# Macaron block on one core: the router with high and low weights side by side as one operand

## The chip, the cores and the metric
One core of one Trainium2 chip. The metric is the device time of one execution in microseconds. Before the change the median of 3 runs is 681.12 us (680.85 to 681.37).

## The reference, cut to what matters
The input x has 16 sequences of 256 tokens with 128 features. It passes through an FFN with a mixture of experts, a mixer (gated convolution and linear recurrence), and the same FFN again, each behind a layer norm and added to x. The part that the change touches is the router of the FFN:

```
logits = tokens @ router_weight.T          # [T, 128] x [128, 32]
scores = sigmoid(logits)
sfc    = scores + router_bias
# two best groups of 8 experts by the sum of their two best; 4 best experts in them
topk_w = scores of the 4, divided by their sum, times 2.5
```

All 32 experts (64 hidden units each) and a shared expert are computed for each token, and an expert's output is weighted by topk_w or by zero.

## The kernel before, in words
**Precision.** Every float32 operand of a large product is split into a high part in fp32r and a low part, the rest. A product is three passes: high with high, high with low, low with high. So it is for the router: for each of the four groups of 128 tokens in a block of 512 it issues three products (L1178 to L1180), with the tokens as the stationary operand and the router's weights, 32 columns, as the moving one; twelve in all, into the PSUM bank `side`.

**Units and slots.** A block is 512 tokens, 8 blocks in all. A unit is one FFN on one block, (1, b) for the first FFN and (4, b) for the second. `ORDER` lists the 16 units: (1,0) to (1,3), then (4,0), (1,4), (4,1), (1,5), (4,2), (1,6), (4,3), (1,7), (4,4) to (4,7). I number them 0 to 15 in that order. A unit has 17 tiles j = 0 to 16 (`NT`): the shared expert and 16 pairs of experts. For a tile TensorE makes a group of three products into `gate_ps` and one into `up_ps` (L1094 to L1096, two banks of each), ScalarE takes silu of gate_ps (L669), VectorE multiplies by the routing weights (`weighted`, L827) and by up_ps (`hid`, L840), ScalarE makes the high part of hid (L677), GpSimd the low part (L562), and TensorE makes three down products (L1152 to L1155), three tiles later. `up_tiles` waits for `hid_done` of tile n-2 before the up group of tile n, and for `weighted_done` of tile n-2 before its gate group.

**Side work.** All that is not a tile is work "beside" it: layer norms, transposes, the router, the routing steps, the mixer, output sums. Tables written by hand (`PREPARE`, `ROUTE4`, `BEGIN`, `END` and others, L315 to L409) give each step a slot: slot 5 on VectorE is between weighted and hid of tile 5, slot 5.5 behind hid of tile 5 (`beside`, L986). On TensorE slot 5 comes behind the tile's up and down products, on ScalarE behind silu of tile 5 and the high part of tile 4. Every engine executes its own list in order. Regular units are those that the tables `MIXER`, `ROUTE4`, `OUTPUT`, `NEXT` describe for (1, b), which route for the second FFN, and `NORM4`, `PROJECT`, `ADD`, `PREPARE` for (4, b), which route for the first FFN.

**The routing chain.** In slot 2 or 3 TensorE runs the router. VectorE then makes 26 small steps (`route_step`, L878), each waiting for the one before: a step away from zero for the logits, reciprocal, score (silu of the logits from ScalarE times the reciprocal), bias, best of groups, ranks, top 8, match_replace, and last `w_tok` (L953). `even(first, last)` spreads them over the half slots. TensorE transposes w_tok (`transpose_route`, L1185), ScalarE copies it (`wT_copy`, L704), and SyncE stores it and broadcasts it to all partitions for the next unit.

**One bank for all.** The PSUM bank `side` serves all side work of TensorE in turn; before a new use TensorE waits until the last one has been read (`side_read`). For the router that is step 2 of the routing chain (`LOGITS_READ`).

**Setup.** Before the units the weights are loaded, transposed and split, and block 0 is routed. The first routing steps lie on VectorE before the low part of batch 3.

Of the kernel before, what the change touches and what calls it, by code (L numbers as in the profile page):

```python
# [111 lines left out]
def macaron_kernel(nc, x, W_in, conv_w, conv_b, a_param, W_out, ln_w, ln_b, router_w, router_b,  # L112
# [4 lines left out]
    with ExitStack() as ctx:  # L117
# [17 lines left out]
        side_te = side_td[:, :, 0:E]  # L135

# [75 lines left out]

        tiny = sb("tiny", [P, TT, E])
# [3 lines left out]
        score = routed[:, 0:128].rearrange("p (t e) -> p t e", t=TT)  # L217
        biased = routed[:, 128:256].rearrange("p (t e) -> p t e", t=TT)
# [56 lines left out]
        logits_ready = {k: sem(f"logits_ready{k}") for k in (1, 4)}  # L275
        logit_silu_done = {k: sem(f"logit_silu_done{k}") for k in (1, 4)}
# [27 lines left out]
        ROUTE = 26  # L304
# [5 lines left out]
        def even(first, last, n=ROUTE):  # L310
# [10 lines left out]
        PREPARE = {"transpose 1": 0, "xT high 1": 1, "xT low 1": 1, "router 1": 2, "silu logits 1": 3,  # L321
                   "route 1": even(2, 12), "weights 1": 13}
        MIXER = {"conv": (0, 0, 0, 0, 0.5, 1.5), "y high": 5, "y low": 5, "mixer out": 9, "mixer sum": 12.5,
                 "stats 3": 13}
        ROUTE4 = {"transpose 4": 0, "xT high 4": 0, "xT low 4": 0.5, "router 4": 3, "silu logits 4": 3,
                  "route 4": even(2.5, 12.5), "weights 4": 13}
# [6 lines left out]
                  "silu logits 1": 4, "route 1": even(4, 12), "weights 1": 13}, 1),  # L333
# [8 lines left out]
                ({"transpose 1": 0, "xT high 1": 0, "xT low 1": 0, "router 1": 1, "silu logits 1": 2,  # L342
                  "route 1": even(1.5, 11.5), "weights 1": 14}, 2),
# [11 lines left out]
                ({"transpose 1": 0, "xT high 1": 0, "xT low 1": 0.5, "router 1": 2, "silu logits 1": 4,  # L355
                  "route 1": even(2.5, 13), "weights 1": 14}, 3),
            ],
            [
                ({"transpose 4": 0, "xT high 4": 0, "xT low 4": 0.5, "router 4": 2, "silu logits 4": 2,
                  "route 4": even(2, 12), "weights 4": 14}, 0),  # L360
# [14 lines left out]
                  "route 4": even(2.5, 12.5), "weights 4": 13}, 4),  # L375
# [11 lines left out]
                  "route 4": even(2, 12), "weights 4": 12}, 5),  # L387
# [3 lines left out]
                ({"transpose 4": 0, "xT high 4": 1, "xT low 4": 1.5, "router 4": 3, "silu logits 4": 3,  # L391
                  "route 4": even(2.5, 12.5), "weights 4": 14}, 6),
# [9 lines left out]
                  "transpose 4": 8, "xT high 4": 9, "xT low 4": 9, "router 4": 10, "silu logits 4": 11,  # L402
                  "route 4": even(10, 14), "weights 4": 15}, 7),
# [27 lines left out]
        LOGITS_READ = 2  # L431
# [220 lines left out]
        def _(act):  # L652
# [40 lines left out]

            def silu_logits(k, b):
                act.wait_ge(route[k], b * ROUTE + 2)
                nc.scalar.activation(logit_silu[:, :, :], logit[:, :, :], ACT.Silu)\
                  .then_inc(logit_silu_done[k], 1)
# [18 lines left out]
            def unit(k, m, before):  # L716

                steps = steps_beside(k, m)
                for j in range(NT):
# [26 lines left out]
                    for b in due(steps, "xT high 2", j):  # L746
                        xT_high(2, b)
                    for b in due(steps, "silu logits 4", j):
                        silu_logits(4, b)
# [28 lines left out]
            for n in range(NBATCH):  # L778
# [11 lines left out]
                if n == 1:  # L790
                    xT_high(1, 0)
                    act.wait_ge(ln_normed[1], 1)
                    act.dma_start(x_ln[:, :, :], x_blk[1]).then_inc(x_ln_loaded, 16)
                if n == 3:
# [14 lines left out]
        def _(dve):  # L809
# [519 lines left out]
```

## Time and profile before

| what | before |
|---|---|
| median of 3 runs | 681.12 us |
| the profiled execution | 680.58 us |
| its span, first to last instruction | 678.4 us |
| TensorE busy (products) | 659.7 us, 97% |
| VectorE busy | 546.8 us, 81% |
| GpSimd busy | 485.4 us, 72% |
| ScalarE busy | 423.2 us, 62% |
| granted clock over the span | 0.995 |

The busy time of TensorE is modelled, since products overlap; distances from start to start tell more. The main loop starts at 28.40 us in the span. An engine that is busy 81% of the time has room on the average, and the table doesn't tell whether it has room where it is waited for.

### The profile page before, as it was taken

Reading aid. Unit: us, or ns where it says so; the run is one execution under the profiler, and the core shown is the slowest. Engines: PE = TensorE matmul, PEld = TensorE weight load, DVE = VectorE, ACT = ScalarE, POOL = GpSimd, SP = SyncE. Lnnn points to the kernel's source line nnn. Section 1 sums busy time; section 2 is a strip of 40 time slices with the busy share of each in tenths; the row PEclk is TensorE's granted clock in tenths of the full one; section 3 lists DMA queues with packets and bytes.
Section 4 is the critical chain, followed back from the end, with each engine's and each line's share of the span. In section 5 each row is a group of like instructions: output and inputs, shape, how many; then the busy total and the mean of one; then the engine's idle time right before and its main releaser. Section 6 shows DMA issues by size and latency. Waiting matters only on the chain. (4 is left out here: it accounts for less than half of the span.)

```text
span 678.4 us, 10540 instructions
## 1 busy us (share of the span) xinstructions
PE 659.7 (97%) x3076; PEld 532.5 (78%) x3076; DVE 546.8 (81%) x1534; ACT 423.2 (62%) x809; POOL 485.4 (72%) x725
## 2 busy tenths in 40 slices
PE   7899999999999999999999999999999999989897
PEld 6778878888888887888887888888878788767685
DVE  5697878989878888889879898788979868867665
ACT  4666576675666656766576755766676575655554
POOL 2167668787686777877777876877786786785673
PEclk8999999999999999999999999999999999999999
DMA  7762908438091734729084471907428092390560
GB/s 187 180 137 63 216 5 190 94 83 186 22 221 43 181 86 100 154 66 214 20 183 101 106 147 53 214 19 169 99 74 179 5 207 58 71 197 2 121 148 15
DMA packets 59721, 78.31 MB, mean 115 GB/s; under 512 B 7664, under 2 KB 27152, under 8 KB 59664
## 3 DMA queue, kind: packets, MB, share of 16 engines
q1 hardware_dynamic: 59136, 77.38, 51.7%
q8 instruction: 24, 0.39, 0.3%
q10 hardware_dynamic: 528, 0.26, 0.2%
q14 instruction: 33, 0.27, 0.1%
HBM read 74.49 MB, written 3.15 MB: 114 GB/s over the span
## 5 line engine op out<-in xcount | busy, mean ns | idle before, releaser
L562 POOL TENSOR_TENSOR hid_lo<-hid,hid_hi 128x256 fp32r<-128x256 f32 x540 | 386.4, 738 | 145.1 <-ACT hid_hi L677 143.3
L827 DVE TENSOR_TENSOR weighted<-gate_ps,raw 128x512 f32<-128x512 f32 x256 | 175.0, 683 | 76.5 <-ACT gate_ps L669 71.2
L669 ACT ACTIVATE gate_ps<-gate_ps 128x512 f32<-128x512 f32 x256 | 148.6, 581 | 125.1 <-PE gate_ps L1096 122.5
L677 ACT ACTIVATE hid_hi<-hid 128x512 fp32r<-128x512 f32 x272 | 170.3, 626 | 57.8 <-DVE hid L840 55.3
L840 DVE TENSOR_TENSOR hid<-weighted,up_ps 128x512 f32<-128x512 f32 x256 | 174.1, 680 | 7.8 <-issue 0.4
L1152 PE MATMUL down_ps<-hid_hi,wt_hi 128*128 128x512 f32 x272 | 107.7, 396 | 2.1 <-ACT ffn_sb L681 2.1
L1155 PE MATMUL down_ps<-hid_lo,wt_hi 128*128 128x512 f32 x272 | 107.9, 397 | 0.2 <-DVE hid_lo L848 0.2
L1153 PE MATMUL down_ps<-hid_hi,wt_lo 128*128 128x512 f32 x272 | 107.5, 395 | 0.0
L1094 PE MATMUL gate_ps<-xT_hi,wt_hi 128*128 128x512 f32 x170 | 71.5, 421 | 2.5 <-DVE wt_lo L814 1.6
L1094 PE MATMUL up_ps<-xT_hi,wt_hi 128*128 128x512 f32 x170 | 68.1, 401 | 0.9 <-DVE hid L840 0.9
L1096 PE MATMUL up_ps<-xT_hi,wt_lo 128*128 128x512 f32 x170 | 67.2, 395 | 0.0
L1095 PE MATMUL gate_ps<-xT_lo,wt_hi 128*128 128x512 f32 x170 | 67.2, 395 | 0.0
L1096 PE MATMUL gate_ps<-xT_hi,wt_lo 128*128 128x512 f32 x170 | 67.2, 395 | 0.0
L1095 PE MATMUL up_ps<-xT_lo,wt_hi 128*128 128x512 f32 x170 | 67.1, 395 | 0.0
L1152 PEld LDWEIGHTS down_ps<-hid_hi,wt_hi 128*128 128x128 f32 x272 | 51.1, 188 | 14.7 <-ACT ffn_sb L681 2.5
L1155 PEld LDWEIGHTS down_ps<-hid_lo,wt_hi 128*128 128x128 f32 x272 | 51.1, 188 | 13.4 <-DVE hid_lo L848 0.9
L1153 PEld LDWEIGHTS down_ps<-hid_hi,wt_lo 128*128 128x128 f32 x272 | 51.1, 188 | 12.3
L1094 PE MATMUL gate_ps<-xT_hi_spare,wt_hi 128*128 128x512 f32 x102 | 42.5, 417 | 0.1
L1094 PEld LDWEIGHTS up_ps<-xT_hi,wt_hi 128*128 128x128 f32 x170 | 31.9, 188 | 11.8 <-DVE hid L840 4.6
L1094 PE MATMUL up_ps<-xT_hi_spare,wt_hi 128*128 128x512 f32 x102 | 40.7, 399 | 0.0
L1096 PE MATMUL gate_ps<-xT_hi_spare,wt_lo 128*128 128x512 f32 x102 | 40.3, 395 | 0.0
L1096 PE MATMUL up_ps<-xT_hi_spare,wt_lo 128*128 128x512 f32 x102 | 40.3, 395 | 0.0
(166 smaller groups left out, 1113.5 us busy)
## 6 DMA issues: line engine op xcount, KB each, us to landing
raw<-wT_hbm SPq DMA_DIRECT2D x64, 640.0 KB, 13.5
raw<-wT_hbm SPq DMA_DIRECT2D x32, 512.0 KB, 7.2
raw<-wT_hbm SPq DMA_DIRECT2D x30, 256.0 KB, 3.9
x_res<-in_L_attn_x SPq DMA_DIRECT2D x8, 256.0 KB, 2.9
x_ln<-in_L_attn_x SPq DMA_DIRECT2D x7, 256.0 KB, 3.3
out_x<-x SPq DMA_DIRECT2D x7, 256.0 KB, 2.3
raw<-in_L_ffn_gate_w SPq DMA_DIRECT2D x4, 256.0 KB, 5.6
raw<-in_L_ffn_up_w SPq DMA_DIRECT2D x4, 256.0 KB, 5.2
```

The source lines that it names most:

```text
L562: last = nc.gpsimd.tensor_tensor(hid_lo[s][:, cols], hid[s][:, cols], hid_hi[s][:, cols].bitcast(F32), ALU.subtract)
L669: nc.scalar.activation(bank[:, :] if j else silu_sb[:, :], bank[:, :], ACT.Silu).then_inc(silu_done, 1)
L677: nc.scalar.activation(hid_hi[s][:, :], hid[s][:, :], ACT.Copy).then_inc(hid_hi_done, 1)
L827: V.tensor_tensor(weighted[j % 2][:, :], gate_ps[n % BANKS][:, :], wb[:, j - 1, :], ALU.mult)\
L840: V.tensor_tensor(hid[n % RING][:, :], factor[:, :], up_ps[n % BANKS][:, :], ALU.mult)\
L1094: nc.tensor.matmul(dst, w, moving_hi, start=start, stop=False)
L1095: nc.tensor.matmul(dst, w, moving_lo, start=False, stop=False)
L1096: return nc.tensor.matmul(dst, w_lo, moving_hi, start=False, stop=stop)
L1152: nc.tensor.matmul(down_ps[:, :], wt_hi[:, w, :], hid_hi[s][:, :], start=(j == 0), stop=False)
L1153: nc.tensor.matmul(down_ps[:, :], wt_lo[:, w, :], hid_hi[s][:, :], start=False, stop=False)
L1155: nc.tensor.matmul(down_ps[:, :], wt_hi[:, w, :], hid_lo[s][:, :], start=False, stop=(j == NT - 1)).then_inc(down_done, 1)
```

## The change
The high and the low part of the router's weights (32 columns each) lie side by side as one operand of 64 columns, so that a group of tokens needs two products: its high part and its low part, each by both. The result has two halves, which are added afterwards: ScalarE copies the second half out of `side` (`copy_low`), and a new first routing step adds the first half to it (`logit_sum`, in the PSUM bank `routed`). The chain has 27 steps. `side` is free after the first of them (`LOGITS_READ` 1). Compared with before, the low parts of the tokens are also multiplied by the low parts of the weights. In the tables, the routing starts one to two slots later; in most units it ends in the same slot.

```diff
@@ route_step
                 if n == 0:
                     dve.wait_ge(logits_ready[k], b + 1)
-                    return st.done(V.tensor_scalar(tiny[:, :, :], side_te, -1e-9, 1e-8, ALU.is_ge, ALU.mult))
-                if n == 3:
+                    dve.wait_ge(logit_low_done[k], b + 1)
+                    return st.done(V.tensor_tensor(logit_sum[:, :, :], side_te, logit_low[:, :, :], ALU.add))
+                if n == 4:
                     dve.wait_ge(logit_silu_done[k], b + 1)
                 st.wait()
                 if n == 1:
-                    st.done(V.tensor_tensor(logit[:, :, :], tiny[:, :, :], side_te, ALU.add))
+                    st.done(V.tensor_scalar(tiny[:, :, :], logit_sum[:, :, :], -1e-9, 1e-8, ALU.is_ge, ALU.mult))
                 elif n == 2:
+                    st.done(V.tensor_tensor(logit[:, :, :], tiny[:, :, :], logit_sum[:, :, :], ALU.add))
+                elif n == 3:
                     st.done(V.reciprocal(logit_inv[:, :, :], logit[:, :, :]))
...
@@ scalar engine
+            def copy_low(k, b):
+
+                act.wait_ge(logits_ready[k], b + 1)
+                nc.scalar.activation(logit_low[:, :, :], side_low, ACT.Copy).then_inc(logit_low_done[k], 1)
...
+                    for b in due(steps, "router 1", j - 1):
+                        copy_low(1, b)
...
@@ setup, vector engine
                 weight_low(n)
+                if n == 0:
+                    dve.wait_ge(w_lo_done, 1)
+                    V.tensor_copy(wt_hi[:, WROUTER, E:2 * E], wt_lo[:, WROUTER, 0:E]).then_inc(router_paired, 1)
...
@@ router, tensor engine
-                w_hi, w_lo = wt_hi[:, WROUTER, 0:E], wt_lo[:, WROUTER, 0:E]
+                w_both = wt_hi[:, WROUTER, 0:2 * E]
                 for t in range(TT):
                     rows = slice(t * P, (t + 1) * P)
-                    x_hi, x_lo = hi_of(k, b)[:, rows], lo_of(k, b)[:, rows]
-                    nc.tensor.matmul(side_te[:, t, :], x_hi, w_hi, start=True, stop=False)
-                    nc.tensor.matmul(side_te[:, t, :], x_hi, w_lo, start=False, stop=False)
-                    last = nc.tensor.matmul(side_te[:, t, :], x_lo, w_hi, start=False, stop=True)
+                    both = side_td[:, t, 0:2 * E]
+                    nc.tensor.matmul(both, hi_of(k, b)[:, rows], w_both, start=True, stop=False)
+                    last = nc.tensor.matmul(both, lo_of(k, b)[:, rows], w_both, start=False, stop=True)
                 last.then_inc(logits_ready[k], 1)
...
@@ tables, PREPARE and ROUTE4 (regular units)
-        PREPARE = {"transpose 1": 0, "xT high 1": 1, "xT low 1": 1, "router 1": 2, "silu logits 1": 3,
-                   "route 1": even(2, 12), "weights 1": 13}
+        PREPARE = {"transpose 1": 0, "xT high 1": 1, "xT low 1": 1, "router 1": 2, "silu logits 1": 5,
+                   "route 1": even(3.5, 12), "weights 1": 13}
...
-        ROUTE4 = {"transpose 4": 0, "xT high 4": 0, "xT low 4": 0.5, "router 4": 3, "silu logits 4": 3,
-                  "route 4": even(2.5, 12.5), "weights 4": 13}
+        ROUTE4 = {"transpose 4": 0, "xT high 4": 0, "xT low 4": 0.5, "router 4": 3, "silu logits 4": 6,
+                  "route 4": even(4.5, 12.5), "weights 4": 13}
```

The other units change in the same way: unit 0 from even(4, 12) to even(5.5, 13.5), its weights from slot 13 to 14; unit 1 from even(1.5, 11.5) to even(2.5, 11.5); unit 2 from even(2.5, 13) to even(3.5, 13); unit 3 from even(2, 12) to even(3.5, 12); unit 11 from even(2.5, 12.5) to even(3.5, 12.5); unit 12 from even(2, 12) to even(2.5, 12), its weights from slot 12 to 13; unit 13 from even(2.5, 12.5) to even(4.5, 12.5); unit 14, with its router in slot 10, from even(10, 14) to even(11.5, 14.5), its weights in slot 15 as before. In setup VectorE runs four routing steps in place of three before the low part of batch 3, ScalarE copies the second half behind the high part of batch 2, and TensorE waits for `router_paired`.

## Rows read from the trace of the kernel before
**Rows 1.** Part 1 of the page: busy us (share of the span) xinstructions.
```profile
PE 659.7 (97%) x3076; PEld 532.5 (78%) x3076; DVE 546.8 (81%) x1534; ACT 423.2 (62%) x809; POOL 485.4 (72%) x725
```

**Rows 2.** Unit 8: stretch, length, busy (x) of PE PEld DVE ACT POOL, clock, DMA.
```profile
345.16:385.10 39.94, 39.94 (x186) 32.27 (x185) 31.88 (x98) 27.78 (x55) 32.36 (x51) 1.00 0.55 121
```

**Rows 3.** Order of time, VectorE, unit 8: start us, us, engine line op out<-in xcount.
```profile
355.77 0.69 DVE L827 TENSOR_TENSOR weighted<-gate_ps,raw 128x512 f32<-128x512 f32 x1 [0.60 <-ACT gate_ps L669]
356.38 0.95 DVE L889 RECIPROCAL routed<-logit 128x128 f32<-128x128 f32 x1
...
359.11 0.69 DVE L827 TENSOR_TENSOR weighted<-gate_ps,raw 128x512 f32<-128x512 f32 x1 [0.57 <-ACT gate_ps L669]
...
359.91 0.68 DVE L840 TENSOR_TENSOR hid<-weighted,up_ps 128x512 f32<-128x512 f32 x1
...
360.71 0.68 DVE L827 TENSOR_TENSOR weighted<-gate_ps,raw 128x512 f32<-128x512 f32 x1
...
361.82 0.68 DVE L840 TENSOR_TENSOR hid<-weighted,up_ps 128x512 f32<-128x512 f32 x1
```

**Rows 4.** Order of time on TensorE, unit 8.
```profile
357.43 0.60 PE L1160 MATMUL side<-ident,ffn_sb 128*128 128x128 f32 x4
...
360.67 0.47 PE L1094 MATMUL up_ps<-xT_hi,wt_hi 128*128 128x512 f32 x1
...
362.85 0.40 PE L1094 MATMUL up_ps<-xT_hi,wt_hi 128*128 128x512 f32 x1
```

**Rows 5.** Order of time on TensorE, the router of unit 8.
```profile
351.92 0.26 PE L1179 MATMUL side<-wt_lo,xT_hi 128*128 128x32 f32 x1
...
353.04 0.26 PE L1180 MATMUL side<-wt_hi,xT_lo 128*128 128x32 f32 x1
```

**Rows 6.** Order of time on TensorE, mixer_out of unit 2.
```profile
122.68 0.27 PE L1192 MATMUL side<-wt_lo,y_hi 128*128 128x128 f32 x1
...
123.80 0.27 PE L1193 MATMUL side<-wt_hi,y_lo 128*128 128x128 f32 x1
```

**Rows 7.** Order of time on TensorE, the router in setup.
```profile
10.58 0.36 PE L1178 MATMUL side<-wt_hi,xT_hi 128*128 128x32 f32 x1 [1.06 <-DVE xT_lo L865]
...
12.93 0.37 PE L1180 MATMUL side<-wt_hi,xT_lo 128*128 128x32 f32 x1
```

**Rows 8.** Groups by line: line engine op out<-in xcount | busy us, mean ns | idle.
```profile
L882 DVE TENSOR_SCALAR tiny<-side 128x128 f32<-128x128 f32 x16 | 4.6, 286 | 5.5 <-PE side L1180 5.4
...
L704 ACT ACTIVATE wT<-side 128x128 f32<-128x128 f32 x16 | 4.3, 266 | 2.5 <-PE side L1185 2.5
```

**Rows 9.** Order of time on VectorE, end of the routing in setup.
```profile
22.30 0.39 DVE L953 SCALAR_TENSOR_TENSOR w_tok<-chosen,routed 128x128 f32<-128x128 f32 x1
```

**Rows 10.** Order of time on ScalarE, unit 8; in brackets idle time and its releaser.
```profile
352.09 0.60 ACT L681 ACTIVATE ffn_sb<-down_ps 128x512 f32<-128x512 f32 x1 [1.89 <-PE down_ps L1155]
...
356.94 1.65 ACT L712 ACTIVATE normed<-x,shift,rstd 128x128 f32<-128x128 f32 x4 [0.45 <-POOL shift L576]
358.50 0.58 ACT L669 ACTIVATE gate_ps<-gate_ps 128x512 f32<-128x512 f32 x1
```

**Rows 11.** Order of time on VectorE, unit 2.
```profile
116.75 0.95 DVE L889 RECIPROCAL routed<-logit 128x128 f32<-128x128 f32 x1
117.61 0.67 DVE L827 TENSOR_TENSOR weighted<-gate_ps,raw 128x512 f32<-128x512 f32 x1
```

**Rows 12.** Order of time on VectorE and TensorE, unit 7.
```profile
338.21 0.37 DVE L953 SCALAR_TENSOR_TENSOR w_tok<-chosen,routed 128x128 f32<-128x128 f32 x1
...
338.72 0.30 PE L1185 MATMUL side<-ident,w_tok 128*128 128x128 f32 x1
```

**Rows 13.** Order of time on TensorE, units 12 and 14.
```profile
539.55 0.30 PE L1185 MATMUL side<-ident,w_tok 128*128 128x128 f32 x1 [0.98 <-DVE w_tok L953]
...
631.91 0.30 PE L1185 MATMUL side<-ident,w_tok 128*128 128x128 f32 x1 [0.84 <-DVE w_tok L953]
```

**Rows 14.** Order of time on VectorE, unit 14.
```profile
618.88 0.29 DVE L882 TENSOR_SCALAR tiny<-side 128x128 f32<-128x128 f32 x1 [0.65 <-PE side L1180]
```

More of the change, by code:

```diff
@@ L135, in macaron_kernel @@
         side_te = side_td[:, :, 0:E]
+        side_low = side_td[:, :, E:2 * E]
         raw = sb("raw", [P, NPAIR * 4, P])
@@ L275, in macaron_kernel @@
         logits_ready = {k: sem(f"logits_ready{k}") for k in (1, 4)}
+        logit_low_done = {k: sem(f"logit_low_done{k}") for k in (1, 4)}
+        router_paired = sem("router_paired")
         logit_silu_done = {k: sem(f"logit_silu_done{k}") for k in (1, 4)}
@@ L296, in macaron_kernel @@
         x3_free = sem("x3_free")
-        ROUTE = 26
+        ROUTE = 27
         def at(table, b):
@@ L332, in macaron_kernel @@
                 ({"norm 1": 0, "normalise 1": 0, "transpose 1": 2, "xT high 1": 2, "xT low 1": 2.5, "router 1": 4,
-                  "silu logits 1": 4, "route 1": even(4, 12), "weights 1": 13}, 1),
+                  "silu logits 1": 7, "route 1": even(5.5, 13.5), "weights 1": 14}, 1),
                 ({"stats 1": 10.5, "meanvar 1": 10.5, "norm 1": 14, "normalise 1": 16}, 2),
@@ L341, in macaron_kernel @@
                 ({"conv": (14, 14.5, 16, 16.5, None, None)}, 0),
-                ({"transpose 1": 0, "xT high 1": 0, "xT low 1": 0, "router 1": 1, "silu logits 1": 2,
-                  "route 1": even(1.5, 11.5), "weights 1": 14}, 2),
+                ({"transpose 1": 0, "xT high 1": 0, "xT low 1": 0, "router 1": 1, "silu logits 1": 4,
+                  "route 1": even(2.5, 11.5), "weights 1": 14}, 2),
                 ({"stats 1": 11.5, "meanvar 1": 12, "norm 1": 14, "normalise 1": 16}, 3),
@@ L354, in macaron_kernel @@
                   "add ln_b": 16}, 1),
-                ({"transpose 1": 0, "xT high 1": 0, "xT low 1": 0.5, "router 1": 2, "silu logits 1": 4,
-                  "route 1": even(2.5, 13), "weights 1": 14}, 3),
-            ],
-            [
-                ({"transpose 4": 0, "xT high 4": 0, "xT low 4": 0.5, "router 4": 2, "silu logits 4": 2,
-                  "route 4": even(2, 12), "weights 4": 14}, 0),
+                ({"transpose 1": 0, "xT high 1": 0, "xT low 1": 0.5, "router 1": 2, "silu logits 1": 5,
+                  "route 1": even(3.5, 13), "weights 1": 14}, 3),
+            ],
+            [
+                ({"transpose 4": 0, "xT high 4": 0, "xT low 4": 0.5, "router 4": 2, "silu logits 4": 5,
+                  "route 4": even(3.5, 12), "weights 4": 14}, 0),
                 ({"conv": (0, 0, 0, 0.5, 1.5, 2.5), "y high": 3, "y low": 5, "mixer out": 8, "mixer sum": 12,
@@ L373, in macaron_kernel @@
                   "meanvar 4": 15, "norm 4": 15, "normalise 4": 16}, 5),
[1 row of a table removed]
-                  "route 4": even(2.5, 12.5), "weights 4": 13}, 4),
[1 row of a table added]
+                  "route 4": even(3.5, 12.5), "weights 4": 13}, 4),
                 ({"copy ffn 4": 2, "transpose ffn 4": 4, "halve ffn": 4, "add ffn 4": 7}, 3),
@@ L385, in macaron_kernel @@
                   "meanvar 4": 14, "norm 4": 14, "normalise 4": 15}, 6),
[1 row of a table removed]
-                  "route 4": even(2, 12), "weights 4": 12}, 5),
[1 row of a table added]
+                  "route 4": even(2.5, 12), "weights 4": 13}, 5),
                 ({"copy ffn 1": 2, "transpose ffn 1": 5, "add ffn 1": 5}, 7),
@@ L390, in macaron_kernel @@
             [
-                ({"transpose 4": 0, "xT high 4": 1, "xT low 4": 1.5, "router 4": 3, "silu logits 4": 3,
-                  "route 4": even(2.5, 12.5), "weights 4": 14}, 6),
+                ({"transpose 4": 0, "xT high 4": 1, "xT low 4": 1.5, "router 4": 3, "silu logits 4": 6,
+                  "route 4": even(4.5, 12.5), "weights 4": 14}, 6),
                 ({"copy ffn 4": 2, "transpose ffn 4": 4, "halve ffn": 5, "add ffn 4": 8}, 4),
@@ L401, in macaron_kernel @@
                   "scale 3": 2, "x2": 3, "stats 4": 4, "meanvar 4": 4, "norm 4": 5, "normalise 4": 6,
-                  "transpose 4": 8, "xT high 4": 9, "xT low 4": 9, "router 4": 10, "silu logits 4": 11,
-                  "route 4": even(10, 14), "weights 4": 15}, 7),
+                  "transpose 4": 8, "xT high 4": 9, "xT low 4": 9, "router 4": 10, "silu logits 4": 12,
+                  "route 4": even(11.5, 14.5), "weights 4": 15}, 7),
                 ({"copy ffn 4": 3, "transpose ffn 4": 4, "halve ffn": 4, "add ffn 4": 4}, 5),
@@ L747, in unit @@
                         xT_high(2, b)
+                    for b in due(steps, "router 4", j - 1):
+                        copy_low(4, b)
                     for b in due(steps, "silu logits 4", j):
@@ L793, in _ @@
                     act.dma_start(x_ln[:, :, :], x_blk[1]).then_inc(x_ln_loaded, 16)
+                if n == 2:
+                    copy_low(1, 0)
                 if n == 3:
@@ L937, in route_step @@
                     st.done(last)
-                elif n == 20:
+                elif n == 21:
                     st.done(V.memset(top8[:, :, TOP:8], FAR))
-                elif n == 21:
+                elif n == 22:
                     V.memset(hold[:, 6:7], 0.0)
@@ L1055, in _ @@
                 if n == 3:
-                    for step in range(3):
+                    for step in range(4):
                         route_step(1, 0, first, step)
                 weight_low(n)
+                if n == 0:
+                    dve.wait_ge(w_lo_done, 1)
+                    V.tensor_copy(wt_hi[:, WROUTER, E:2 * E], wt_lo[:, WROUTER, 0:E]).then_inc(router_paired, 1)
                 if n == 1:
@@ L1062, in _ @@
             dve.wait_ge(pool_const, 5)
-            for step in range(3, ROUTE):
+            for step in range(4, ROUTE):
                 route_step(1, 0, first, step)
@@ L1271, in _ @@
             weights(2)
-            pe.wait_ge(w_lo_done, 1)
+            pe.wait_ge(router_paired, 1)
             router(1, 0)
```

48 lines of the change are left out of this document (25 added, 23 removed), and 4 rows, old and new, of the table END.

## The prediction
> **What bounds the kernel now.** I read the page first. TensorE is busy 659.7 of 678.4 us [rows 1]; the reader is to see that no other engine comes near. Next came the busy time by stretch: in the unit from 345.16 to 385.10 TensorE has work for all 39.94 us, VectorE for 31.88 [rows 2]. So in the middle of the run a microsecond taken from TensorE is a microsecond gained, as long as nobody else becomes late. Third, the order of time on TensorE, to get distances from start to start, since its busy time is modelled. Last, VectorE and ScalarE in one unit of each kind, to see how close they are to being late. That last view decides here: a product group of up_ps for tile n+2 starts only when hid of tile n is written, and in this unit the group of tile 6 starts at 360.67, 0.08 us after hid of tile 4 ends (359.91 + 0.68) [rows 3, 4]. VectorE is busy only 80% there, and still it has no room at that spot.
>
> **What TensorE saves.** Between the second and the last of the twelve router products lie ten steps and 1.12 us (351.92 to 353.04): 0.112 us each with 32 moving columns [rows 5]. mixer_out's products have 128 moving columns and the same distance, 122.68 to 123.80 in ten steps [rows 6]. A product of 64 columns lies between two kinds that cost the same, so I take 0.112. Four fewer are 0.45 us a router, 6.7 us over the fifteen routers of the main loop.
>
> The Trainium skill, TensorE: Matmul & The Clock Gate, section Back-to-back issue gap, puts a product of 1 to 64 columns, at the full clock, at about 60 cycles with a floor of 25 ns. By that table the four products would be worth 0.1 us a router and 1.6 us in all; the same page's section on LDWEIGHTS has a load of 128 columns at 107 ns, which is what the rows agree with, so I keep 0.112.
>
> **Setup.** The twelve products are 0.214 us apart here (10.58 to 12.93, eleven steps), and start when xT_lo is written [rows 7]. The added copy of 32 columns on VectorE sits before that; nearest rows are 128-column operations of 0.27 and 0.29 us [rows 8], so 0 to 0.3, and VectorE waits for ScalarE after it: I take 0, and 0.3 if that cover is gone. The router ends 0.86 earlier, but ScalarE's copy and the new sum come behind it (0.3 each, with their hand-overs), and what follows is VectorE's routing chain, which ends with w_tok at 22.69 [rows 9] and holds the main loop's start. I take -0.1 (bounds -0.86 and +0.3).
>
> **What is added beside it.** Per router: one ScalarE copy (nearest row 0.27 us) and one VectorE step (0.29) [rows 8]. The copy waits for the logits at the ScalarE slot after the router's; by then gate_ps of that slot, a later product, has been waited for, so it stalls nobody. The cost is in the table of slots. Routing starts 1 to 2 slots later and ends, in most units, where it did, so 27 steps share fewer slots. Behind each step on VectorE's queue stand weighted and hid, and TensorE waits for both.
>
> **A unit of kind (4, m), of which four are regular (units 4, 6, 8, 10).** Take unit 8. ScalarE copies the last FFN result at 352.09, as soon as TensorE has ended the last down product, which is before the router; its later work is held by that and by GpSimd (normalise waits until 356.94), so silu of tile 4 runs at 358.50 whatever the router costs [rows 10], and weighted of tile 4 stays at 359.11. Before the change five routing steps are over by then, the reciprocal of 0.95 us among them (356.38), in gaps in which VectorE had to wait for ScalarE in any case (even so 0.57 idle before 359.11) [rows 3]. After the change only the sum is over, and the other steps come where VectorE has no gap.
> - Slot 4.0 will hold two steps instead of one. One step makes weighted to hid 0.80 (359.11 to 359.91), two make it 1.11 (360.71 to 361.82) [rows 3]. hid of tile 4 moves from 359.91 to 360.22, its end to 360.90, the up group of tile 6 to 360.98: 0.31 later than now.
> - Slot 4.5 will hold the reciprocal, 0.86 from its start to the next operation's (116.75 to 117.61) [rows 11], in place of a 0.20 step. A weighted or hid takes 0.60 until the next start (355.77 to 356.38) [rows 3], so weighted of tile 5 is at 360.22 + 0.60 + 0.86 = 361.68. Two steps follow: hid of tile 5 at 362.79, ends 363.47. The up group of tile 7, now at 362.85 [rows 4], starts at 363.55: 0.70 late. A product that has waited is 0.47 long instead of 0.40 [rows 4], so 0.78.
> - Later slots add less than the slack has grown. The transposes of the FFN result wait for the sum in side: weighted and hid at 355.77 and 356.38, sum over at 357.27, against 357.43 - 0.45 = 356.98 [rows 3, 4]; this wait of 0.3 is inside the 0.78.
> So each such unit is 0.78 longer instead of 0.45 shorter: +3.1. Lower end -0.45 each, if the order on VectorE leaves the gap open.
>
> **A regular unit of kind (1, m) (units 5, 7, 9).** Routing moves from slots 2.5 to 12.5 to 4.5 to 12.5. Here VectorE has idle time from tile 6 on. What binds is the end: w_tok ends at 338.58 and its transpose starts at 338.72, right behind [rows 12]. Match_replace moves from slot 11.0 to 11.5, but VectorE is ahead by then, and I get w_tok 0.4 earlier. The score step may wait up to 1 us for ScalarE, which takes the silu of the logits behind halve_ffn at slot 6; I count that as hidden, since weighted and hid of tile 6 are early (if not, 0.3). -0.4 each, -1.2; bounds -0.45 and +0.3 (the added step, nothing earned).
>
> **The four first units.** In unit 0 the routing weights move to slot 14 with steps up to 13.5; counted through, w_tok ends about when TensorE passes slot 14 now: +0.1. Units 1 to 3 have no tight hid and have their weights at slot 14 already, so the broadcast to the next unit has its time: -0.4 each. Sum -1.1.
>
> **The last five.** Unit 12 waits 0.98 us for w_tok at 539.55 [rows 13]; with the transpose a slot later that wait goes, but late next is the chain over x2 to normalise 4, which only moves with the unit's start: -0.4. Units 11 and 13: -0.35 each. In unit 14 VectorE paces everything from the first routing step at 618.88 (it had waited for the router) to the transpose at 631.91 [rows 13, 14], 12.9 us of unbroken work with eight weighted/hid in it. After the change step 0 may only run at slot 11.5: after weighted and hid of tile 11, about 621.2. From there: the same 8.1 us of routing, 0.3 for the sum, six weighted/hid at 0.6 (12.9 - 8 x 0.6 = 8.1): w_tok ends at 633.2, the transpose is at about 633.35, 1.45 late. Unit 15 follows unchanged. Sum +0.3.
>
> **Sum.** -0.1 - 1.1 + 3.1 - 1.2 + 0.3 = +1.0 on the profiled execution's 680.58 (span 678.4 and 2.2 around it), 681.6. The runs' median is 681.12, 0.54 above that execution, so 682.1.
>
> **Rivals.**
> - *The cover holds.* If VectorE's extra work in units 4, 6, 8 and 10 finds room, they give 0.45 each instead of taking 0.78: 4.9 less, 677.2. For it: VectorE's 80% [rows 2]. Against: the 0.08 us behind hid of tile 4.
> - *All of it arrives.* 6.7 + 0.86 off: 673.6. It needs units 0 and 14 too to be free of VectorE.
> - *Slower: the end of routing binds everywhere.* The transpose of w_tok waits in every unit, as it now does in units 12 and 14 [rows 13]. It decides from the point at which w_tok ends after TensorE's slot, which is 0.45 sooner than now. The eight units that I have at -0.35 to -0.4 then keep nothing: +3.2, 685.3; with the added step on the same chain up to 687.8. For it: the transpose at 338.72 right behind w_tok [rows 12]; against: idle time in mid-unit.
> - *A 64-column product costs two of 32.* Excluded by the 128-column rows [rows 6].
>
> **How the numbers follow.** 0.2% is 1.36 us, about what can be told from no change here. Forecast case 0.50, own range 680 to 684; within it 0.10 faster, 0.50 same, 0.40 slower. Cover holds 0.20, all arrives 0.05, slower 0.20, rest 0.05 near no change. Faster 0.05 + 0.20 + 0.05 = 0.30; same 0.25 + 0.05 = 0.30; slower 0.20 + 0.20 = 0.40. The range 676.5 to 685.8 takes in the first and the third rival and leaves out the second and the tails.
>
> **What would show it.** Right: router products 0.112 apart, eight of them; in units 4, 6, 8, 10 waits of the up groups of tiles 6 and 7 for hid, some 1.2 us of them; the reciprocal between hid 4 and weighted 5; unit 14 longer by 1.4. Wrong: up groups there without a wait, or regular (1, m) units no shorter, or weighted of tile 4 earlier in its unit than 13.95 us after the first gate product.

## The result, and the profile after

The changed kernel takes 689.23 us (median of 4 runs, 688.78 to 690.77), the kernel before 681.25 in the same session (4 runs, 680.85 to 681.69): ratio 1.0121, 95% interval 1.0104 to 1.0139. It is 1.2% slower. The forecast was 682.1 in a range of 676.5 to 685.8, that is 1.0 over the median, with a chance of 0.40 for slower. Its sign came out and an eighth of its size, and the measured time lies 3.4 above the range. The profiled execution took 689.0 us, its span is 687.2 against 678.4.

Part 1 of the page after, engine busy us (share of the span) xinstructions, beside [rows 1]:

```profile
PE 658.7 (96%) x3012; PEld 522.5 (76%) x3012; DVE 550.7 (80%) x1551; ACT 427.1 (62%) x825; POOL 485.4 (71%) x725
```

TensorE has 64 products fewer and its busy time fell by only 1.0 us, while the time in which it had no product grew from 18.7 to 28.5 us. The products themselves did what the change says: there are eight, and from the second to the last in unit 8 six steps take 0.67 us, 0.112 each, as with 32 columns [rows 5]. Order of time on TensorE, the router of unit 8, after:

```profile
355.21 0.27 PE L1201 MATMUL side<-wt_hi,xT_lo 128*128 128x64 f32 x1
...
355.88 0.28 PE L1201 MATMUL side<-wt_hi,xT_lo 128*128 128x64 f32 x1
355.99 0.48 PE L1116 MATMUL gate_ps<-xT_hi,wt_hi 128*128 128x512 f32 x1
```

Units from first gate product to first gate product, us (unit 15 to the start of TensorE's last transpose, behind which 3.4 us follow in both; the main loop starts at 28.40 before and at 27.72 after):

```
unit        0     1     2     3     4     5     6     7     8     9    10    11    12    13    14    15
before  37.26 40.06 41.30 39.39 39.90 39.46 39.93 39.46 39.93 39.47 39.93 42.88 40.71 40.26 45.81 40.85
after   38.07 40.37 41.65 39.40 41.17 39.25 41.18 39.63 41.17 39.25 41.17 42.48 40.17 41.41 47.35 42.36
change  +0.81 +0.31 +0.35 +0.01 +1.27 -0.21 +1.25 +0.17 +1.24 -0.22 +1.24 -0.40 -0.54 +1.15 +1.54 +1.51
```

They add up to +9.5, less 0.7 for the setup: the 8.8 of the span. In four rows by stretch of the trace after, units 8, 9, 13 and 15 (stretch, length, then the engines' busy time as in [rows 2]):

```profile
348.45:389.62 41.17, 40.61 (x182) 31.45 (x181) 31.68 (x99) 27.85 (x56) 32.19 (x51) 1.00 0.50 114
389.61:428.87 39.26, 39.09 (x184) 31.72 (x182) 35.02 (x94) 23.81 (x45) 28.61 (x40) 1.00 0.56 122
552.68:594.10 41.42, 40.24 (x181) 31.83 (x180) 32.55 (x88) 27.45 (x53) 29.80 (x44) 1.00 0.49 105
641.45:683.81 42.36, 39.63 (x171) 30.73 (x169) 24.59 (x37) 21.53 (x39) 25.60 (x35) 1.00 0.49 106
```

In unit 8 VectorE is busy for 31.68 us, less than the 31.88 before [rows 2], and the unit is still 1.24 longer: VectorE has one small step more there and no more work in sum; it does it later. Three totals of TensorE's waits over the whole run after (engine, line, what it waited for: us, times, longest) show where this is felt:

```profile
PE side L1206 <- DVE w_tok L972: 5.5, 6, 3.0
...
PE side L1182 <- DVE routed L899: 2.3, 6, 0.7
...
PE up_ps L1116 <- DVE hid L856: 1.5, 6, 0.6
```

Line 1206 is the transpose of w_tok, line 1182 are transposes into `side` that stand behind the new sum (L899), line 1116 is the first product of a group.

### The profile page after: what moved, and what is told of

It reads as the page before. It is cut to its first block and busy times, and to the rows that moved or that the text cites. A ratio compares the mean times of both kernels' runs of the same rounds, so it can differ in the third digit from the quotient of the medians.

```text
span 687.2 us, 10461 instructions
## 1 busy us (share of the span) xinstructions
PE 658.7 (96%) x3012; PEld 522.5 (76%) x3012; DVE 550.7 (80%) x1551; ACT 427.1 (62%) x825; POOL 485.4 (71%) x725
## 5 line engine op out<-in xcount | busy, mean ns | idle before, releaser
L1174 PEld LDWEIGHTS down_ps<-hid_hi,wt_hi 128*128 128x128 f32 x272 | 51.2, 188 | 14.5 <-ACT ffn_sb L686 2.5
L1117 PE MATMUL gate_ps<-xT_lo_spare,wt_hi 128*128 128x512 f32 x102 | 40.4, 396 | 0.0
```

The source lines that it names most:

```text
L1117: nc.tensor.matmul(dst, w, moving_lo, start=False, stop=False)
L1174: nc.tensor.matmul(down_ps[:, :], wt_hi[:, w, :], hid_hi[s][:, :], start=(j == 0), stop=False)
```

## The experiments

Theory A says that the loss is VectorE's schedule: routing starts one to two slots later, is packed closer, and TensorE has to wait for it. Rivals: B, the added step costs wherever it stands; C, products of 64 columns give nothing in this program; D, the wait for ScalarE's copy is what costs. "The old table" is that of the kernel before, "the new table" that of the change. The first four runs build the change up piece by piece on one chip, on which the kernel before takes 682.49 (14 runs, 680.87 to 684.35).

**The products alone.** The kernel before with eight products and nothing else. It routes by the first half of the logits, so it leaves the second half out.

```diff
-                    nc.tensor.matmul(side_te[:, t, :], x_hi, w_hi, start=True, stop=False)
-                    nc.tensor.matmul(side_te[:, t, :], x_hi, w_lo, start=False, stop=False)
-                    last = nc.tensor.matmul(side_te[:, t, :], x_lo, w_hi, start=False, stop=True)
+                    nc.tensor.matmul(both, hi_of(k, b)[:, rows], w_both, start=True, stop=False)
+                    last = nc.tensor.matmul(both, lo_of(k, b)[:, rows], w_both, start=False, stop=True)
```

> The kernel before with its router in eight products of 64 columns and nothing else: 26 routing steps from the first half of the logits, the old table, no copy on ScalarE. The second half (x times the low part of the weights) isn't added, so its time is that of the products alone. Theory A (the loss is VectorE's: routing that starts later, is packed closer and has to be over sooner): the four products' saving arrives, 15 x 0.45 us, so 674 to 675. Rival C (products of 64 columns, or the saving on TensorE, are worth nothing in this program): 681.

Measured 678.81, ratio 0.9941 (0.9921 to 0.9962): 3.7 us less, not 6.7. It lies between A's 674 to 675 and C's 681. The products are worth something, against C, but A's premise that all of their saving arrives is wrong too. The units say where it stops (by stretch, units 8 and 9 of this kernel):

```profile
344.06:383.99 39.93, 39.93 (x182) 31.64 (x180) 31.88 (x98) 27.77 (x55) 32.41 (x51) 1.00 0.54 119
383.99:423.02 39.03, 39.03 (x183) 31.66 (x182) 34.98 (x93) 23.46 (x44) 28.46 (x40) 1.00 0.55 119
```

Unit 9 is shorter by the whole 0.44, unit 8 is 39.93 long as before. Silu of tile 4 starts 13.35 us after the unit's first gate product (357.41) as it did before (358.50 - 345.16 = 13.34) [rows 10], behind a normalise that waits for GpSimd. Order of time on ScalarE, products alone, unit 8, which starts at 344.06:

```profile
355.85 1.65 ACT L713 ACTIVATE normed<-x,shift,rstd 128x128 f32<-128x128 f32 x4 [0.46 <-POOL shift L577]
357.41 0.58 ACT L670 ACTIVATE gate_ps<-gate_ps 128x512 f32<-128x512 f32 x1
```

The gate product of tile 4 is 0.44 us earlier than before (9.03 us into the unit in place of 9.47), that of tile 8 is not (19.10 and 19.09). So in the (4, m) units the four products saved are worth nothing at all.

**The change with twelve products.** The changed kernel, its router issued as three products of 32 columns per group of tokens, one of them into the second half.

> The changed kernel with everything of its table, its ScalarE copy and its sum, but the router again in twelve products of 32 columns (four of them into the second half). Theory A: about half of the products' saving is seen in it, since the waits that replaced it begin earlier by as much; 691 to 693. Rival C: 689, no change. If the products' saving is fully there and the added cost independent of it, 696.

Measured 693.22, ratio 1.0154 (1.0131 to 1.0177), against 1.0121 for the change: 0.2 above A's 691 to 693, and neither C's 689 nor the 696 of a saving that is fully there. Units 0 to 13 take 569.0 us in place of 566.4, so the products are worth 2.6 here and 2.9 over the old table (559.9 before, 557.0 with the products alone). Unit 8 is 41.18 with twelve as with eight.

**The sum without the copy, old table.**

```diff
+        side_halves = side_td[:, :, 0:2 * E].rearrange("p t (h e) -> p t e h", h=2)
...
+                    return st.done(V.tensor_reduce(logit_sum[:, :, :], side_halves, AX.X, ALU.add))
```

> Eight products, 27 routing steps, but the two halves are added by one VectorE reduction that reads both from the bank, so no copy on ScalarE is needed and routing starts where it did before: the old table (the 27 steps over the same slots; one silu of logits a slot later). Theory A: 675 to 677.5. Rival B (the added step itself is what costs, wherever routing starts): 683 to 689. Rival C: 681 to 682.

**The same, new table.** The changed kernel's table, without its `copy_low`.

> The same reduction in place of copy and addition, but with the changed kernel's table, so that it differs from the changed kernel only in the ScalarE copy and from the reduction with the old table only in where the steps stand. Theory A (the table costs): 687 to 689. Rival D (the wait for the ScalarE copy costs, not the table): 676 to 680.

Measured 681.75 with the old table (ratio 0.9990, 0.9978 to 1.0001) and 689.00 with the new one (1.0104, 1.0077 to 1.0130). There are 7.3 us between two kernels that execute the same operations and differ only in where they stand. 689.00 is the upper end of A's 687 to 689. D falls: with the copy (1.0121) or without it, the time is the same within the intervals. But with the old table the time is 4 us above A's 675 to 677.5, at the 681 to 682 that was C's (which the products alone exclude), so the added step costs something too. Units 8, 9 and 13 by stretch, old table, then new:

```profile
344.50:384.43 39.93, 39.81 (x181) 31.76 (x180) 31.87 (x99) 27.85 (x55) 32.43 (x51) 1.00 0.54 118
384.43:423.47 39.04, 39.04 (x184) 31.66 (x182) 35.29 (x94) 23.48 (x44) 28.47 (x40) 1.00 0.56 123
547.86:587.70 39.84, 39.74 (x182) 31.91 (x180) 32.51 (x88) 26.97 (x52) 29.24 (x42) 1.00 0.45 98
```

```profile
349.02:390.19 41.17, 40.48 (x181) 31.43 (x180) 31.79 (x99) 27.67 (x55) 32.17 (x51) 1.00 0.51 113
390.19:429.46 39.27, 39.09 (x184) 31.68 (x182) 35.77 (x94) 23.64 (x44) 28.54 (x40) 1.00 0.56 120
553.16:594.74 41.58, 40.27 (x182) 31.79 (x180) 32.59 (x88) 27.30 (x52) 29.80 (x44) 1.00 0.50 107
```

Unit 8 with 27 steps over the old slots is 39.93: the added step finds room there. Moved later it costs 1.24 in unit 8 and 1.74 in unit 13.

**Only the middle of the table.** The reduction, with `PREPARE` and `ROUTE4` of the changed kernel.

> The reduction with the old table (681.75), into which only the two entries of the regular middle units of the changed kernel's table are put (routing from slot 3.5 to 12 and from 4.5 to 12.5; the first four and the last five units keep the old ones). Theory A: only units 4 to 10 change, (4, m) from 39.93 to 41.17 and (1, m) from 39.03 to 39.27, 4 x 1.24 + 3 x 0.24 = 5.7 us: 686.5 to 688.5. Rival F (the table costs mostly in the first and last units, where the waits add up differently): under 685.

Measured 689.14 (4 runs, 688.16 to 690.79), ratio 1.0122 (1.0106 to 1.0139). Units 4 to 10 are as A says: 41.18, 39.29, 41.18, 39.26, 41.16, 39.26, 41.17, that is 5.7. Rival F (under 685) falls. The total lies 0.6 above the range. Against the reduction with the old table three units differ in the profile without any change of their entries. Unit 2 is 1.0 longer and the last one 0.9, both because the fourth load of the routing weights lands later (10.64 us into the unit in place of 8.72, and 13.39 in place of 12.52). Unit 14 is 1.0 shorter, since with the whole old table the granted clock was 0.50 for 3.4 us there (602.6 to 606.0), behind a stop of TensorE of 2.1 us, and here it stayed at 1.00 behind the same stop. Every profile has this stop. In four the clock fell behind it (the change with twelve products, the reduction with the old table, the constant guard, and that with the short warm-up), in the others it did not.

**One guard step less.**

```diff
-                    st.done(V.tensor_scalar(tiny[:, :, :], logit_sum[:, :, :], -1e-9, 1e-8, ALU.is_ge, ALU.mult))
...
-                    st.done(V.tensor_tensor(logit[:, :, :], tiny[:, :, :], logit_sum[:, :, :], ALU.add))
+                    st.done(V.tensor_scalar(logit[:, :, :], logit_sum[:, :, :], 1e-8, None, ALU.add))
```

> Eight products, the halves added by the reduction, and the guard against a logit of zero in one step instead of two (1e-8 is added always, not only where the logit is at least -1e-9), so that routing has 26 steps again, over the old table. Theory A (with the old table the number of steps decides): the 2.9 us between the runs with 26 and 27 steps over the old table come back, 677.5 to 679.5. Rival E (the reduction that reads both halves from the bank costs, not the number of steps): 681 to 682.

Measured 680.12 (12 runs, 678.80 to 681.80), before 681.61 (25 runs), ratio 0.9977 (0.9966 to 0.9988): between the two ranges, 0.6 above A's. Units 0 to 13 take 557.4 us against 559.7 with 27 steps: the step costs 2.3, of which 1.1 in unit 12 (41.51 to 40.38), where TensorE waits 1.8 us for w_tok in place of 1.0, and 0.8 in unit 0 (37.58 to 36.79), where with 27 steps hid comes late for two up groups, here the second of them on TensorE:

```profile
57.69 0.50 PE L1102 MATMUL up_ps<-xT_hi,wt_hi 128*128 128x512 f32 x1 [0.17 <-DVE hid L843]
```

B is right in these units and nowhere in the middle. The medians show less than the profiles: 681.75 to 680.12, in two sessions whose kernels before are 0.9 apart. Against the products alone (557.0) the reduction costs 0.4.

**The wait of slot 9.** In the changed kernel, one number: `"add ffn 1": 8.5` becomes `8`.

> The changed kernel with one entry of its table changed: the addition of the FFN result on VectorE at slot 8.0 instead of 8.5 in the middle units of kind (4, m). In the changed kernel TensorE's transposes of slot 9 wait 0.3 for it. If this wait is a loss of its own: 1.2 less over the four units, 687.5 to 688.3. If the time is lost again at the next late tile: 689.

Measured 689.30, ratio 1.0104 (1.0086 to 1.0123): the second case, lost again. The transposes of slot 9 start without a stop now, and unit 8 is 41.12 in place of 41.17: the wait came back one tile later, at the mixer's gate product in slot 10 (0.42 from start to start). So this entry does not pace the unit. That VectorE's unbroken work does is what the rows on unit 8 below say, and no run shows it by itself.

**Normalise a slot later.** In the kernel with the constant guard, `"normalise 2": 3` in `PROJECT` becomes `4`.

> The kernel with the constant guard, with the normalise of the mixer (1.65 us on ScalarE, behind GpSimd's shift) a slot later, so that the silu of tile 4 no longer stands behind it in the four middle units of kind (4, m). If this is why these units are 39.93 long with eight products as with twelve: they shorten to 39.5, 1.8 in all, 676 to 677.5. If something else holds them: 678 to 679, or above if normalise is then late itself.

Measured 681.62 (12 runs, 679.23 to 686.21), ratio 1.0005 (0.9987 to 1.0024), so 1.5 above the constant guard. The (4, m) units are 40.25, 40.27, 40.25 and 40.22: longer by 0.3, the last case of the expectation. Order of time on ScalarE, unit 8, which starts at 343.50:

```profile
354.74 0.58 ACT L672 ACTIVATE gate_ps<-gate_ps 128x512 f32<-128x512 f32 x1
...
357.24 1.64 ACT L715 ACTIVATE normed<-x,shift,rstd 128x128 f32<-128x128 f32 x4
358.78 0.57 ACT L672 ACTIVATE gate_ps<-gate_ps 128x512 f32<-128x512 f32 x1
```

Silu of tile 4 did come free, 11.24 us into the unit instead of 13.35, but now the normalise holds silu of tile 5 (15.28 in place of 14.38). So the normalise holds whatever stands behind it; that the unit would shorten without it is not shown.

**Instruction fetches.** The profile lists some DMA queues as "instruction"; I call their packets fetches. That queue 8 carries TensorE's program is inferred from the counts below. A transfer lands when its data have arrived, and landing times count from its issue. With eight products the last unit was 42.16, 42.50 and 42.36 long in the profiles of three kernels that leave its table untouched (the products alone, the reduction, the change), against 40.85. Its tile weights come over HBM: TensorE's transpose of w_tok, ScalarE's copy, a store, then eight loads. DMA in a stretch of 3 to 3.5 us from before the last store, first the kernel before, then the changed one (issues: KB each, median us from issue to landing):

```profile
q1 hardware_dynamic: 144, 0.07, 7.5%
...
wT_hbm<-wT SPq DMA_DIRECT2D x1, 64.0 KB, 1.5
```

```profile
q1 hardware_dynamic: 144, 0.07, 7.2%
q8 instruction: 1, 0.02, 2.1%
...
wT_hbm<-wT SPq DMA_DIRECT2D x1, 64.0 KB, 3.1
```

Queue 8 moves 24 pieces of 16 KB in every kernel here. Counted in TensorE's instructions (weight loads, products and the 137 waits and the like between them), in the eight kernels with 6161 of them the last piece but one begins at the 5811th to 5817th, and the last store 6 or 8 instructions ahead of it. With twelve products the store is at 5933 or 5937, far from one. The stop that the late store can cause is that of VectorE for the fourth load, at tile 5. In all profiles but the last one below the last unit is 40.8 us where this load landed up to 10.8 us into the unit (the kernel before, the change with twelve products, the short warm-up), and longer by whatever it landed behind 10.9: 42.36 with a landing at 12.40 in the changed kernel. The pair that differs only in the products shows the store's part: with the new table the fourth load took 8.94 us with twelve products and 8.95 with eight, the store landed in 1.52 and 3.10, and the unit is 40.84 and 42.36. Two more kernels test the fetch.

60 waits that are already met, on TensorE in the setup:

> The kernel with the constant guard plus 60 waits that are already met, on TensorE early in the setup. They compute nothing; they move the places at which TensorE's program is fetched back to about where they are with twelve products. If the late landing of the last store of the weights (3 us where the kernel before has 1.5) comes from the fetch that falls on it, the store lands in 1.5 us and the last unit is 1.2 to 1.5 shorter: 676.5 to 678. If the landing varies by itself: no difference to the constant guard.

Measured 679.90 (8 runs), ratio 0.9969 (0.9958 to 0.9980). The landing was 3.0 again and the last unit 42.60: missed. The 60 waits made 30 instructions, and the store moved to the 5839th and the fetch to the 5847th, together. So the fetch did not stay at its count, and whether it causes the late landing can't be told from this run.

`WARM = 2` in place of 14, 24 instructions fewer:

> The kernel with the constant guard, with 2 transposes instead of 14 in the warm-up of TensorE at the very start. It has 24 TensorE instructions fewer ahead of everything, so that the fetch of TensorE's program that now falls 8 instructions behind the last transpose of the routing weights falls some 32 behind it, 3 us later. If that fetch is what makes the store land late: the store lands in 1.5 us and the last unit is near 41 instead of 42.2 to 43.0; 678 to 679, if the setup isn't longer. If not: last unit 42 or more, 680.

Measured 678.11 (5 runs, 677.94 to 679.06), before 681.46, ratio 0.9955 (0.9942 to 0.9967). This is the case that was expected of the fetch. The store is at 5785, the fetch at 5807, 22 instructions behind it (32 were expected), and the last unit is 40.84, with its fourth load in at 10.79. Its DMA from 630.7 to 634.5, and the unit by stretch:

```profile
q8 instruction: 1, 0.02, 2.1%
...
wT_hbm<-wT SPq DMA_DIRECT2D x1, 64.0 KB, 1.5
```

```profile
631.90:672.74 40.84, 39.29 (x170) 30.85 (x169) 24.80 (x37) 21.69 (x40) 25.87 (x36) 1.00 0.49 111
```

The fetch is in this stretch too, but behind the store's landing. The main loop starts at 27.80 (27.65 with 14), so the gain isn't the setup's. Unit 14, with the clock at half for 3.4 us in both, is as long as with 14 (46.60 and 46.58).

The kernel before, unchanged:

> The kernel before once more, for a second profile. If the store's landing follows from where the fetches fall, all but the seventh store land in 1.5 us again, the last among them, and the last unit is 40.85 again. If the landing varies by itself, one of them differs.

680.34 us. The last unit is 40.84, all stores land in 1.5 us but the seventh (2.4; it was 2.8 in the first profile), which has a fetch on it both times. All profiles together have 224 of these stores. 38 landed after more than 2.2 us, and every one of them had a fetch that began 0.06 to 1.3 us behind its issue (32 of 16 KB, 6 of 8 KB); a fetch of 16 KB that began between 0.4 us ahead of a store and 1.1 behind it left none at 1.5. A late store alone doesn't make the unit longer: with the reduction and the new table the last store landed in 3.0 and the unit was 40.87 all the same, since the fourth load took 7.60 us where it took 8.95 in the changed kernel, and was in at 10.90. Why a load of the same size takes 7.5 us in one execution and 10.4 in another is open.

The changed kernel with `WARM = 2`:

> The changed kernel with 2 warm-up transposes in place of 14, and nothing else. If 1.5 us of its loss are the fetch of TensorE's program on the last store: the store lands in 1.5 us instead of 3.1, the last unit is 40.85 long instead of 42.36, and the time is 687.3 to 688 against 689.2. If the saving in the run with the constant guard came from a shorter setup: the last unit stays above 42 and the main loop starts earlier.

Measured 690.12 (4 runs, 689.79 to 691.57), ratio 1.0127 (1.0110 to 1.0144): no gain, missed. The store did land in 1.5 us and the stop at tile 5 is gone, yet the last unit is 41.59 and unit 14 is 49.20 in place of 47.35. TensorE's granted clock fell in the 3.05 us wait for w_tok (at 638.2) and was back at 645.0. By stretch, then TensorE in order of time:

```profile
638.00:644.90 6.90, 5.62 (x14) 4.49 (x15) 3.65 (x8) 2.05 (x5) 2.86 (x4) 0.51 0.26 61
```

```profile
639.28 0.45 PE L1206 MATMUL side<-ident,w_tok 128*128 128x128 f32 x1 [3.05 <-DVE w_tok L972]
639.38 0.77 PE L1116 MATMUL gate_ps<-xT_hi,wt_hi 128*128 128x512 f32 x1
639.95 0.63 PE L1117 MATMUL gate_ps<-xT_lo,wt_hi 128*128 128x512 f32 x1
```

0.51 is the level of 1.2 GHz; the products are 0.43 apart instead of 0.23 for some 13 of them, 2.6 us, which is what units 14 and 15 lost and more than the landing gave back. The changed kernel has the same wait and kept its clock there in its profile (639.21, below). Nor did the fetch move off the store here as it did with the short warm-up above: it is at 5787, again 8 instructions behind the store at 5779, and began 1.64 us behind it because these 8 ran at half the clock. So two kernels of the same length have it 20 instructions apart, and what places a fetch is not settled. The 1.5 us of the last unit are shown in the profiles, and as time won back with the constant guard (680.12 to 678.11), not in this kernel.

**The best version** that adds both halves is the one with eight products, the sum by reduction, the constant guard, the old table and the short warm-up: 678.11, 0.45% under the kernel before and 1.6% under the changed one (0.9955 / 1.0121 = 0.9836).

## Why the prediction was wrong

Units 0 to 13 as a sum of pieces, each the difference of two kernels in their profiled executions (two profiles of the kernel before differ by 0.1 in this sum, but a late load can add 1.0 to one unit, as above): 559.9 before; products alone -2.9; reduction in place of the read of one half +0.4; the 27th step +2.3; the table +6.7; copy and addition in place of the reduction 0.0; 566.4 after. Then +1.5 in unit 14, +1.5 in unit 15, -0.7 in the setup.

**TensorE's saving: price right, value wrong.** 0.112 us a product held for 64 columns. The figure in the Trainium skill, TensorE: Matmul & The Clock Gate, section Back-to-back issue gap (about 60 cycles for up to 64 columns), is not what these rows show; each product here has its own load of 128 columns. But I gave 0.45 to every unit without a tight hid, "a microsecond taken from TensorE is a microsecond gained", and had silu of tile 4 fixed in the (4, m) units without drawing the consequence. This is the first step that failed: by the modelled busy time TensorE is busy all through such a unit, 39.94 of 39.94 us with 186 products and 39.93 of 39.93 with 182, and still does not set its length. With nothing else changed, units 2, 3, 4, 6, 8, 10 and 11 keep nothing, and 2.9 us of 6.3 arrive in units 0 to 13. The rival "the cover holds" was mispriced by this: it gives 0 in these units (39.93 with 27 steps over the old slots), not -0.45.

**The (4, m) units: right up to the gate group of tile 8, then the step "Later slots add less than the slack has grown" failed.** Order of time on VectorE, unit 8 after, beside [rows 3]; the unit starts at 348.45, 3.29 later than before:

```profile
362.39 0.69 DVE L843 TENSOR_TENSOR weighted<-gate_ps,raw 128x512 f32<-128x512 f32 x1 [1.66 <-ACT gate_ps L674]
...
363.52 0.68 DVE L856 TENSOR_TENSOR hid<-weighted,up_ps 128x512 f32<-128x512 f32 x1
364.12 0.95 DVE L908 RECIPROCAL routed<-logit 128x128 f32<-128x128 f32 x1
364.98 0.67 DVE L843 TENSOR_TENSOR weighted<-gate_ps,raw 128x512 f32<-128x512 f32 x1
...
366.10 0.68 DVE L856 TENSOR_TENSOR hid<-weighted,up_ps 128x512 f32<-128x512 f32 x1
```

Taken back by 3.29 these are 359.10, 360.23, 360.83, 361.69 and 362.81; predicted were 359.11, 360.22, reciprocal behind it, 361.68 and 362.79. Where VectorE had idled 0.57 us ahead of weighted 4 it now idles 1.66, because routing that had filled the gaps was still to come. The gate group of tile 8 is 19.88 us into the unit, before 19.09: 0.79 late, predicted 0.78. But from 362.39 VectorE works without a gap to 379.28, 16.9 us where it had 15.9 before, and the slack never grows. The next rows on TensorE and VectorE:

```profile
360.79 0.66 PE L1182 MATMUL side<-ident,ffn_sb 128*128 128x128 f32 x4 [0.31 <-DVE routed L899]
366.83 0.50 PE L1116 MATMUL up_ps<-xT_hi,wt_hi 128*128 128x512 f32 x1 [0.16 <-DVE hid L856]
```

```profile
380.87 0.87 DVE L869 BATCH_NORM_STATS2 stats<-x 128x6 f32<-128x128 f32 x4 [1.59 <-POOL x L606]
381.66 0.27 DVE L968 TENSOR_REDUCE wsum<-chosen 128x4 f32<-128x132 f32 x1
...
382.66 0.37 DVE L972 SCALAR_TENSOR_TENSOR w_tok<-chosen,routed 128x128 f32<-128x128 f32 x1
```

The sum of the weights, which stood ahead of the wait for GpSimd's x2, has slipped behind it, and w_tok ends 34.58 us into the unit against 33.17 (377.97 + 0.36 - 345.16). 0.31 more at slot 9 and 0.15 at w_tok, with the 0.79, make the 1.24 of the unit. Over the four units that is +5.0 where +3.1 was forecast.

**(1, m) units.** -1.2 forecast, -0.3 measured, in the three. Here the third rival was the true one. w_tok ends 32.67 us into units 5 and 9, 0.2 earlier than the 32.88 before where 0.4 was forecast, and the products alone and the old table have it at 32.45. So its transpose is waited for: the old table has 39.03 (all of the saving), the new one 39.27, and unit 7 of the changed kernel, where w_tok ends at 33.06, has 39.63. "Regular (1, m) units no shorter" was one of the signs of being wrong, and unit 7 shows it.

**The first units.** -1.1 forecast, +1.5 measured. Units 2 and 3 have nothing of the saving (above). Units 1 and 2 are 0.3 longer each; no run takes that apart. Unit 0 waits for w_tok, which I had "about when TensorE passes":

```profile
61.46 0.30 PE L1206 MATMUL side<-ident,w_tok 128*128 128x128 f32 x1 [1.07 <-DVE w_tok L972]
```

**Unit 13.** -0.35 forecast, +1.15 measured. Routing starts at slot 4.5 there, and the transposes of the FFN result are at slot 4 of TensorE; one bank serves both, and 0.9 of the loss is this wait (the rest lies at slots 0 and 1):

```profile
566.15 0.29 DVE L899 TENSOR_TENSOR routed<-side,logit_low 128x128 f32<-128x128 f32 x1
566.49 0.66 PE L1182 MATMUL side<-ident,ffn_sb 128*128 128x128 f32 x4 [0.70 <-DVE routed L899]
```

I had counted this wait in unit 8 (0.3) and not where the table puts the read behind the next user. Units 11 and 12 came about as forecast (-0.40 and -0.54, for -0.35 and -0.4).

**Unit 14.** +1.45 forecast, +1.54 measured:

```profile
639.21 0.30 PE L1206 MATMUL side<-ident,w_tok 128*128 128x128 f32 x1 [3.05 <-DVE w_tok L972]
```

45.11 us into the unit, before 43.57 [rows 13]. The wait is longer than before since TensorE has nothing left by then.

**Unit 15.** 0 forecast ("Unit 15 follows unchanged"), +1.51 measured, by the late landing of the last store and of the fourth load behind it:

```profile
653.94 0.69 DVE L843 TENSOR_TENSOR weighted<-gate_ps,raw 128x512 f32<-128x512 f32 x1 [3.40 <-DMA raw<-wT_hbm]
```

**The signs.** Those of being right came out: eight products 0.112 apart, the reciprocal between hid 4 and weighted 5, unit 14 longer by 1.5, and in unit 8 the up groups of tiles 6 and 7 start 0.41 and 0.55 us after the product before them in place of 0.23. They could not see the rest of a (4, m) unit, 0.45 of its 1.24, and nothing of units 0, 13 and 15. That the sign of the forecast was right says little. Its +1.0 is what +4.5 of losses (3.1 and 1.45) leave over 3.5 of savings, and of these savings only those of the setup, of units 5 and 9 in part, and of units 11 and 12 came; had the losses been read 1.1 lower, which is less than they were off, the sign would have been wrong.

## What to carry to other kernels

A saving on the busiest engine counts only in the stretches that aren't held by something else; take one anchor per stretch (here silu of tile 4) and ask whether it moves. When work is shifted later on an engine with idle time, count the idle time that it had filled: 7 of the 8 us were lost by moving the same operations, and none that shows by the added copy. And where a result goes over HBM just in time, look at what else the DMA queues carry at that moment, instruction fetches included: a change elsewhere in the program can put one there.

## What the hardware showed

A fetch of 16 KB of instructions that began in the 1.1 us behind the issue of a store of 64 KB went with a landing of 2.1 to 3.5 us in place of 1.5. In the eight kernels with 64 products fewer and the long warm-up one such fetch began 0.8 to 1.0 us behind the last store of the routing weights, which with twelve products has none near. In seven of them the last unit is longer, by 1.3 us in the least and 3.0 in the worst profile (43.90, with the addition a half slot earlier, where the fourth load was slow too, 10.4 us), and in one it is as long as before. A reduction that reads both halves of the logits from the bank takes the place of a copy and an addition at no cost (566.35 us for units 0 to 13 against 566.38).
